# Re-dealing the patch stage of a small vision transformer kernel: row sums on column groups, matmuls without a reader at the start, statistics amid the last part, masks on GpSimd

## The reference, cut to what matters

```
h = patch_tokens(x)                      # five shifted copies of x, 16x16 patches: 3840 values per token
    tn = (t - mean(t)) * rsqrt(var(t) + 1e-5) * gamma + beta
    h  = tn @ W[3840,192] + b
h = concat(cls_tok, h)                   # 37 positions x 16 images
h = h + attention(layernorm(h))          # 12 heads of 16, a bias of the relative position added to the scores
h = h + ffn(layernorm(h))                # a shared SiLU block of width 768, and 8 experts of width 192, top 2
```

## Time and profile before

| | us |
|---|---|
| runs, median (lowest to highest) | 155.68 (154.63 to 157.39) |
| the profiled execution | 155.41 |
| its span | 153.5 |
| PE busy | 134.4 (88%) |
| DVE busy | 108.5 (71%) |
| ACT busy | 91.0 (59%) |
| POOL busy | 50.6 (33%) |

### The profile page before, as it was taken

The page is one execution under the profiler, slowest core; times in us unless marked ns, Lnnn a source line. Parts: engine busy times, 40 slices in busy tenths (PEclk is TensorE's granted clock), DMA queues, the critical chain, the costliest instruction groups (busy, mean ns, idle before and its releaser), DMA issues.

```text
span 153.5 us, 4141 instructions
## 1 busy us (share of the span) xinstructions
PE 134.4 (88%) x1630; PEld 105.3 (69%) x1630; DVE 108.5 (71%) x280; ACT 91.0 (59%) x219; POOL 50.6 (33%) x63
## 2 busy tenths in 40 slices
PE   0239999999999989995679999998899999999991
PEld 0115887794478878984458868886587778787881
DVE  6389959989896999547475999857947623723753
ACT  0398695975997674683279868555544444444430
POOL 7000000500001432000005324586568386477430
PEclk9999999999999999999999999999999999999999
DMA  4999992780002323004995000485000000000003
GB/s 121 398 337 393 286 301 57 241 320 8 0 0 59 71 71 67 4 0 117 394 395 228 0 4 6 112 317 208 0 0 4 0 2 0 4 0 2 0 4 119
DMA packets 9941, 17.85 MB, mean 116 GB/s; under 512 B 2758, under 2 KB 6162, under 8 KB 9922
## 3 DMA queue, kind: packets, MB, share of 16 engines
q1 hardware_dynamic: 9562, 17.25, 34.0%
q10 hardware_dynamic: 360, 0.34, 0.8%
HBM read 16.63 MB, written 0.96 MB: 115 GB/s over the span
## 4 chain that ended last, share of the span: by engine, by line
PE 68%; DVE 10%; ACT 8%; issue 6%; ACTq 3%; POOL 2%; DVEq 0%; POOLq 0%
PE PS L684 20%; PE PS L714 10%; PE PS L458 4%; PE PS L408 3%; PE PS L495 3%; PE PS L573 3%; PE PS L542 3%; PE PS L431 2%; PE PS L429 2%; PE PS L432 2%; POOL vhl L1061 2%; DVE vhl L1448 2%; PE PS L556 2%; PE PS L395 2%; PE PS L599 2%
## 5 line engine op out<-in xcount | busy, mean ns | idle before, releaser
L1070 POOL TENSOR_TENSOR kq<-vhl,kq 128x296 f16<-128x296 f32 x35 | 28.7, 821 | 43.5 <-ACT kq L987 43.5
L1448 DVE SCALAR_TENSOR_TENSOR vhl<-PS,vhl 128x296 f32<-128x296 f32 x36 | 16.8, 465 | 19.9 <-POOL vhl L1061 10.5
L980 ACT ACTIVATE vhl<-PS 128x296 f32<-128x296 f32 x36 | 14.9, 415 | 24.3 <-PE PS L684 22.9
L987 ACT ACTIVATE kq<-vhl 128x296 f16<-128x296 f32 x36 | 16.0, 446 | 6.6 <-DVE vhl L1448 6.4
L1061 POOL TENSOR_TENSOR vhl<-vhl,xs 128x296 f32<-128x296 f32 x14 | 12.6, 899 | 5.6 <-issue 4.9
L1046 POOL TENSOR_TENSOR piece<-stage,piece 128x768 f16<-128x768 f32 (+1 forms) x3 | 4.6, 1525 | 22.7 <-DVE mx L1315 22.7
L1437 DVE TENSOR_TENSOR vhl<-vhl,xs 64x296 f32<-64x296 f32 (+1 forms) x18 | 10.2, 566 | 2.6 <-ACT vhl L980 2.4
L684 PE MATMUL PS<-XAh,piece 128*128 128x296 f16 x48 | 9.5, 290 | 1.6 <-ACT XAh L865 0.7
L684 PE MATMUL PS<-XAh,slab 128*128 128x296 f16 x48 | 10.0, 291 | 0.9 <-DVE vhl L1448 0.9
L431 PE MATMUL PS<-whl,xhl 128*128 128x193 f16 (+1 forms) x40 | 10.5, 263 | 0.0
L429 PE MATMUL PS<-whl,xhl 128*128 128x193 f16 (+1 forms) x40 | 10.5, 263 | 0.0
(11 more groups left out here) (233 smaller groups left out, 375.9 us busy)
## 6 DMA issues: line engine op xcount, KB each, us to landing
slab<-in_w_inner_dram SPq DMA_DIRECT2D x3, 960.0 KB, 9.5
xs<-gate_rows_dram SPq DMA_DIRECT2D x8, 296.0 KB, 5.7
xs<-in_x_inner_dram SPq DMA_DIRECT2D x3, 592.0 KB, 10.5
stage<-in_f_a_dram SPq DMA_DIRECT2D x2, 768.0 KB, 4.9
stage<-in_f_b_dram SPq DMA_DIRECT2D x2, 768.0 KB, 6.8
stage<-in_f_d_dram SPq DMA_DIRECT2D x2, 576.0 KB, 8.2
xhl<-in_f_a_dram SPq DMA_DIRECT2D x1, 768.0 KB, 9.3
xhl<-in_f_b_dram SPq DMA_DIRECT2D x1, 768.0 KB, 10.6
```

Of the source, the lines that this page charges most:

```text
L980: A(silu[:, i % 2, :], PS[:, 3 + 2 * (i % 2), 0:HALF], ACT.Silu, scale=1.0 / XW).then_inc(S["a_silu"], 1)
L987: A(ah[:, f % ABUF, half * HALF:(half + 1) * HALF], hf[:, i % 3, :], ACT.Copy).then_inc(S["a_ah"], 1)
L1070: G.tensor_tensor(al[:, f % ABUF, cols], hf[:, i % 3, :], ah[:, f % ABUF, cols], ALU.subtract).then_inc(S["g_al"], 1)
L1448: V.scalar_tensor_tensor(out=hf[:, i % 3, :], in0=PS[:, 4 + 2 * (i % 2), 0:HALF], scalar=SH / XW, in1=src[:, i % 2, :], op0=ALU.mult, op1= ...
```

## The change

The patch stage is dealt anew between the engines, and what ran beside its end is moved.

- **PE, start:** 12 and 8 matmuls of 512 columns that nobody reads (`warm_up`, bank 1), before and behind `beta_rows(0)`.
- **PE, sums:** `square_rows` puts its four products on four column groups of 32. The 193rd column goes; `mean_rows` makes the pixels' row sums on four column groups, and `column_sums` puts the column sums there too. Both need a last sum over the groups.
- **PE, order:** sums of later parts go ahead of `patches` of earlier ones. In the last part tile after tile is finished; the statistics (now 10 products of one column, not 5) stand behind tile 1 and the sum of the column sums (`column_total`) behind tile 2.
- **ACT:** six small DMAs and five waits less at the start (they move to SP), but its table DMAs wait for two memsets on POOL. `weights_high(2)` and `pixels(3)` come ahead of `squares(2)`. The ring's first weights go to DVE. The splits of the attention's weights are spread over the waits of the stage's end. `ffn_high(0)` and `(1)` of piece 0 stand behind the last copies of the first layernorm and ahead of `kq_high(0)`; the prescaled copies go.
- **DVE:** the mask work goes. The row sums are copied out (`mrows`). `queries_keys_low(1)`, `(2)` and all `values_low` now stand between the steps of the layernorm. All six `ffn_low` of piece 0 are on DVE, between and behind the differences.
- **POOL:** makes the masks after the table's DMAs; makes no low halves of piece 0.

```diff
             def square_rows(i):
...
-                for half in (0, 1):
-                    for j in (2 * i, 2 * i + 1):
-                        q = 32 * (j % 4)
+                for j in (2 * i, 2 * i + 1):
+                    for half in (0, 1):
+                        q = 64 * half + 32 * (j % 2)
...
+            def mean_rows(i):
...
+                for n, x in enumerate((xh, xl)):
+                    for j in (2 * i, 2 * i + 1):
+                        for half in (0, 1):
+                            q = 64 * half + 32 * (j % 2)
+                            last = mm(PS[q:q + 32, half, 0:HALF], wh[0:K, j, D:D + 1].to_broadcast([K, 32]),
+                                      x[0:K, j, half * HALF:(half + 1) * HALF], start=(i == 0 and n == 0),
+                                      stop=(i == 3 and n == 1), skip_group_check=True)
+            def column_sums(i):
...
+                for j in (2 * i, 2 * i + 1):
+                    for n, w in enumerate((wh, wl)):
+                        q = 64 * (j % 2) + 32 * n
+                        last = mm(PS[q:q + 32, 2, D:2 * D], oneh[0:K, :].to_broadcast([K, 32]), w[0:K, j, 0:D],
+                                  start=False, stop=(i == 3), skip_group_check=True)
+            def warm_up(n):
+                for _ in range(n):
+                    mm(PS[:, 1, :], oneh[:, :].to_broadcast([P, P]), oneh[:, :].to_broadcast([P, 512]), start=True,
+                       stop=True)
...
-            for i in range(4):
-                beta_rows(i)
-                square_rows(i)
-                patches(i)
+            pe.wait_ge(S["v_one"], 1)
+            warm_up(12)
+            beta_rows(0)
+            warm_up(8)
+            square_rows(0)
+            beta_rows(1)
+            mean_rows(0)
+            patches(0)
+            square_rows(1)
+            mean_rows(1)
+            beta_rows(2)
+            patches(1)
+            mean_rows(2)
+            patches(2)
+            square_rows(2)
+            beta_rows(3)
+            mean_rows(3)
+            square_rows(3)
+            weights_ready(3)
+            column_sums(3)
             for t in range(TILES):
+                if t == 2:
+                    statistics()
+                if t == 3:
+                    column_total()
+                patch(CHUNKS - 2, t)
+                patch(CHUNKS - 1, t).then_inc(S["p_main"], 1)
...
-            pe.wait_ge(S["a_aw"], 15)
-            pe.wait_ge(S["v_awl"], 15)
...
+                if f == 0 and i in (0, 2, 4):
+                    pe.wait_ge(S["a_aw"], 5 + 5 * (i // 2))
+                    pe.wait_ge(S["v_awl"], 5 + 5 * (i // 2))
...
             first_shift(2)
             pixels(2)
+            weights_high(2)
+            pixels(3)
             squares(2)
-            first_shift(3)
-            pixels(3)
-            weights_high(2)
+            squares(3)
             weights_high(3)
-            squares(3)
...
+            queries_keys_high(0)
+            act.wait_ge(S["p_cp"], 1)
+            A(bc[:, :], PS[:, 2, 0:2 * D], ACT.Copy).then_inc(S["a_bw"], 1)
+            act.wait_ge(S["p_cc"], 1)
+            A(csum[:, :], PS[:, 0, 0:D], ACT.Copy, scale=1.0 / 32).then_inc(S["a_cs"], 1)
...
             root(0)
-            ffn_high(0, 0)
-            ffn_high(0, 1)
-            prescaled(0)
+            bias_rows()
+            queries_keys_high(1)
+            queries_keys_high(2)
             root(1)
-            prescaled(1)
-            ffn_high(0, 5)
-            prescaled(5)
+            for k in range(3):
+                values_high(k)
             copies(0, range(3))
             root(2)
             high_parts(0, (1, 2, 0), 0)
             A(small[:, 46, 0:1], one[:, :], ACT.Exp)
             copies(0, (3, 4))
+            ffn_high(0, 0)
+            ffn_high(0, 1)
             kq_high(0)
...
+            pool.wait_ge(d_tab, 128)
+            G.tensor_tensor(tab6[:, :, :], tabs[:, :, 0:6], tabs[:, :, 6:12], ALU.add).then_inc(S["g_mk"], 1)
...
-            ffn_low(0, 1)
-            ffn_low(1, 2)
-            ffn_low(5, 3)
...
+            centred(2)
             residual(0, add_patches, (0, 1, 2))
             variances(1)
+            queries_keys_low(1)
+            rsqrt(1)
+            for t in (3, 4):
+                centred(t)
+            normed(0, range(3))
             residual(0, add_patches, (3, 4))
-            rsqrt(1)
-            normed(0, range(3))
             variances(2)
+            queries_keys_low(2)
...
-            values_low(1)
-            values_low(2)
+            for k in range(3):
+                values_low(k)
...
             differences(0)
             keys_third(5)
-            ffn_low(0, 2)
+            ffn_low(0, 0)
             differences(1)
-            ffn_low(0, 3)
+            ffn_low(0, 1)
             differences(2)
             normalise(0)
-            ffn_low(0, 4)
             differences(3)
+            ffn_low(0, 2)
             normalise(1)
             normalise(2)
+            for q in (3, 4, 5):
+                ffn_low(0, q)
```

More of the change, by code:

```diff
@@ L434, in patches @@
[L434 to L446 removed]
+                        patch(j, t)
@@ L460, in _ @@
             pe.wait_ge(S["a_aw"], 5)
[L461 removed]
+            for name, count, n in (("v_stat", 5, 6), ("v_h", 3, 6), ("v_stat", 9, 6), ("v_stat", 10, 4)):
                 pe.wait_ge(S[name], count)
@@ L933, in _ @@
             ffn_high(0, 4)
+            ffn_high(0, 5)
             def ctx_high(i):
```

275 lines of the change are left out of this document (141 added, 134 removed).

## The result

| | before | after |
|---|---|---|
| runs, median (lowest to highest) | 155.47 us (154.63 to 157.39), 4 runs | 162.73 us (160.29 to 167.28), 4 runs |
| the profiled execution, its span | 155.41, 153.5 | 167.28, 165.4 |
| mean granted clock over the span, by run | 0.998 in the profile | 0.957, 0.957, 0.947, 0.917 |
| ratio after / before | | 1.033, 95% interval 1.025 to 1.041 |

The forecast was 157.0 us, with 154.2 to 158.8 as its range and 0.12 for slower by over 2%. The change costs 3.3%: it was wrong. (The ratio leaves out the two runs with the lowest clock; the profile is one of those, so its losses are larger than the ratio's.)

The account below looks back on a forecast made before the run. Bound by a chain of waits through PE to the first scores at 46.49 us, then alternating between PE and DVE. 155.41 + 1.45 (first scores late) + 0.1 (DVE's added splits) = 157.0 us; range 154.2 to 158.8, 8 in 10.

Parts of the forecast that it names:

- last part's products start: End of the patch stage on PE: start at 25.8 to 26.0 us, against 29.3 before.
- root(0) out: First layernorm's root on ACT, behind its table load: out at 32.1 us against 34.75, 2.6 us early.
- first residual starts: DVE, behind the root and bias rows: start at 33.7 us, not 35.75, 2.05 us early.
- normed, tiles 0 to 2, starts: DVE in the first layernorm: start at 38.65 us instead of 40.16, 1.5 us early despite an added split.
- `kq_high(0)` starts: ACT, behind `ffn_high(0)` and `(1)` (1.57 us): start at 46.4 us against 44.80, 1.6 us late.
- first scores start: `scores(0)` on PE, behind 1.5 us of key and query copies: 47.9 us against 46.5, 1.45 us late.
- from there to the root of the second layernorm: Behind the first scores: DVE gains three splits, which overrun its 2.14 us wait for PE by 0.1 us.
- so I take it as high from the first squares on: PE at the start: `warm_up` raises the clock before the squares, so 5 us at the lower clock become 2.5.
- the clock falls back: Rival: PE's clock drops in the 1.7 us wait after `warm_up`, 2.2 us late, 159.2 us; chance 0.12.
- The gain survives: Rival: DVE reaches the last normed tiles by 42.5 us, keeping some of 2.05 us; at most 153.4; chance 0.22.
- Masks against folds: Rival: POOL's masks (about 2.3 us) slow DVE's folds by up to 1.2 us, 157.7 us; chance 0.12.
- Warm-up: PE's start: 12 unread matmuls, some 5 us in which nobody waits; 5 us at the lower clock become 2.5.

Follow-up runs that it names:

- e7: The changed kernel plus 16 unread matmuls of 512 columns: amid the statistics, ahead of the bias rows and around the first values; median 159.6 us, ratio 1.017 to 1.030.
- e6: The kernel before without its 27 unread `keep_warm` matmuls; median 160.6 us, against 155.9 for the kernel before.
- e14: e9 with the bias rows ahead of the root and the splits of `WB` ahead of the statistics; median 158.7 us, ratio 1.009 to 1.024.
- e18: e14 with unread matmuls in PE's waits up to 80 us and six amid the statistics; median 157.3 us, ratio 1.004 to 1.016.
- e4: The kernel before plus the 20 unread matmuls of `warm_up`; median 157.0 us, ratio 1.006 to 1.014.
- e9: The changed kernel with column total ahead of statistics, root's table loaded early, `ffn_high(0)`, `(1)` in ACT's waits, `high_parts` ahead of `root(2)`; median 159.4 us, ratio 1.009 to 1.029.

## Why the prediction was wrong, step by step

| step | forecast | after, profiled | e7, less the 0.8 us of its fills |
|---|---|---|---|
| last part's products start (ahead of the fills) | 25.8 to 26.0 | 27.0 | 26.5 |
| csum copied out by ACT | 30.6 | 32.8 | 31.1 |
| root(0) out | 32.1 | 34.3 | 32.6 |
| first residual starts | 33.7 | 36.7 | 34.3 |
| normed, tiles 0 to 2, starts | 38.65 | 42.3 | 39.2 |
| `kq_high(0)` starts | 46.4 | 50.0 | 46.9 |
| first scores start | 47.9 | 51.6 | 48.6 |
| from there to the root of the second layernorm | 23.2 + 0.1 | 29.4 | 23.4 |

- **The sum of the order was right to 0.6 us**: this order takes 157.6 us at the clock that the kernel before had, for the 157.0 forecast. The 0.6 is there already where the last part starts, and stays to the first scores. PE's sums were put too short: for a part's squares 0.55 us where they took 0.70, for its row sums 0.35 where they took 0.43, for the column sums 0.2 where they took 0.27. The 157.6 rests on one run of a version with fills; no run of the changed kernel itself was without falls.
- **The step that failed** is the first: "so I take it as high from the first squares on". True of the squares (0.71 us for eight at 11.58), and false of the 150 us behind them. Every duration in the sum came from a trace whose strip is full, and I carried the clock over with them, though the change takes work from PE, puts narrow products in its place and moves copies so that it waits. Every run of the changed kernel was at the lower clock for 14 to 27 us. Of the 7.2 us between the medians (155.5 and 162.7) some 2.1 are the order, by e7's figure, and the other 5.1 the clock. In the two runs with least of it (160.3 us, 14 us low) the clock's part is 2.7 us by the difference from 157.6, and 4.6 by the slope of 0.34: the slope of one kernel doesn't carry over to another as it stands.
- **The rival "the clock falls back"** named the mechanism, but at the wrong place (the gap behind warm_up) and as one fall of 2.2 us. Its chance of 0.12 was that of a gap, and it should have been that of a kernel with 27 matmuls that hold the clock and a change that thins what is around them. I had read those matmuls as work that costs nothing, and did not ask what they hold up; e6 answers that with 4.7 us.
- **"The gain survives"** fell for the reason given: DVE's work is on the path, and e14 and e18 lose a lead of 1.4 to 1.6 us at `normed` before the scores.
- **Masks against folds.** Seen, and small: the second part's eight folds (L1215) took 3.10 us beside POOL's masks, for 2.72 in the kernel before, 0.4 us and not up to 1.2. POOL's mask work itself was mis-sized: 5.2 us (9.53 to 15.3), for the 2.3 of my estimate.
- **Warm-up**: 5 us at the lower clock were to become 2.5. In e4 PE gains 1.4 us by the end of the patches, 0.26 of it reaches the statistics, and the runs are slower for the fall that comes with it.
- **Missed on the way**: ACT's `root(2)` in front of `XAh` holds PE for 1.11 us. It was hidden behind `ffn_high`, so it changed nothing in the sum, but it was there to be read in the order.

## What to carry to other kernels

Where unread matmuls stand in a tuned kernel, its clock is part of the design: before pricing a change that takes work from TensorE, mark the stretches that they cover and ask what the change leaves there, and test with a handful of unread matmuls before anything else. A gain at one engine's early step is worth what the engine behind it has free; DVE had nothing. When runs of one kernel scatter more than those of another, look at the mean granted clock by run: it told more than the medians did.

## What the runs showed of the hardware

- The clock can fall while PE counts as busy: 3.00 of 3.00 us from 26.00 to 29.00, ahead of the fall at 29.9. The Trainium skill (TensorE: Matmul & The Clock Gate, section "Why this matters for your kernels") asks for no long idle gaps between bursts; here the one wait of PE between 12 us and the fall was of 0.93 us, and the clock fell all the same. What stands in the stretch ahead of it is narrow work: one-column products (1.07 us for five, 28.03 to 29.10) and sums of 32 columns. That the narrow work is the reason isn't shown. In e6 the fall does lie in a long wait (5.69 us).
- A fall costs less than its length: 0.34 us for each us at the lower clock in the kernel before.
- Every load of a table took 1.28 us, in all the profiles, and the next instruction of ACT that was ready started 0.01 to 0.02 us behind it; pulled ahead of other copies (e9, e14) the load left the path.
- Whether a fall comes varies from run to run of one program: 37 of 55 runs of the kernel before had none, and of 13 runs on one chip four fell. Why the later ones (64 to 91 us in the changed kernel), on code that the change doesn't touch, come, these runs don't settle.
